# Rows and a column load in the Q stage, statistics turned by VectorE, V's second half, the roots, the index chain and the jump moved: a two-layer kernel on one core

## What is computed

```python
x = x + attn(layernorm(x), Wq, bq, Wk, bk, Wv, bv)
x = x + (einsum('bsi,oi->bso', layernorm(x), weight * scale[:, None]) + bias)
```

```python
q, k, v = heads(h @ Wq + bq), heads(h @ Wk + bk), heads(h @ Wv + bv)
# local: query block i (128 tokens) sees keys i*128-64 .. (i+1)*128+64
ctx = softmax(mask(q_block @ k_window.T / 8)) @ v_window
# global: token 0, the 62 tokens of largest |q| of this head, token 1023
idx = [0, top_k(norm(q), 62), 1023]
ctx[idx] = softmax(q[idx] @ k.T / 8) @ v          # all keys
```

## Time and profile before

| | us |
|---|---|
| median of 3 runs | 2128.19 (2123.09 to 2137.35) |
| profiled execution | 2130.37 |
| its span | 2128.8 |
| TensorE matmuls busy | 2018.6 (95%) |
| VectorE busy | 1521.7 (71%) |
| ScalarE busy | 1002.0 (47%) |
| GpSimd busy | 602.6 (28%) |
| mean granted TensorE clock | 0.970 |

### The profile page before, as it was taken

One profiled execution on the slowest core, in us unless ns is written; L12 is line 12 of the kernel. 1 busy time (PEld: TensorE's weight loads), 2 busy tenths in 40 slices (PEclk: granted clock), 3 DMA queues, 4 the chain that ended last, 5 costly groups with the idle time before them and its releaser, 6 DMA issues.

```text
span 2128.8 us, 36751 instructions
## 1 busy us (share of the span) xinstructions
PE 2018.6 (95%) x11264; PEld 1680.7 (79%) x11264; DVE 1521.7 (71%) x2907; ACT 1002.0 (47%) x1435; POOL 602.6 (28%) x478
## 2 busy tenths in 40 slices
PE   6997999989989999889899998999999989999999
PEld 6875878877868788778687887887888878888887
DVE  5596778763888778637887686578777877666664
ACT  4224756673246666733365666534676672000000
POOL 2332214123342232133422321344223203212121
PEclk9998999989989999899899999999999999999999
DMA  3427787653367767443578775425767656333331
GB/s 139 125 76 147 155 132 164 124 116 114 109 145 166 130 148 155 100 121 114 132 149 131 155 137 125 114 87 117 162 140 181 139 105 190 130 138 128 138 128 69
DMA packets 539685, 280.78 MB, mean 132 GB/s; under 512 B 439120, under 2 KB 504726, under 8 KB 539536
## 3 DMA queue, kind: packets, MB, share of 16 engines
q1 hardware_dynamic: 511440, 186.76, 41.8%
q0 software_dynamic: 23776, 76.63, 12.0%
q10 hardware_dynamic: 4320, 15.73, 1.8%
HBM read 122.73 MB, written 51.44 MB: 82 GB/s over the span
## 4 chain that ended last, share of the span: by engine, by line
PE 77%; DVE 11%; issue 5%; DMA 4%; ACT 2%; SPq 1%; DVEq 0%; POOL 0%; ACTq 0%; POOLq 0%
PE proj L647 39%; PE proj L807 15%; PE pv L765 10%; PE pv L787 3%; PE turn L753 2%; PE score L753 2%; DMA p_turned<-p_parts 2%; DVE top_val L1456 2%; DVE top_idx L1458 2%; DVE x_norm L1460 2%; PE score L779 1%; PE turn L796 1%; DMA v_turned<-q_sq 1%; DVE q_sq L1422 1%; PE proj L925 1%
## 5 line engine op out<-in xcount | busy, mean ns | idle before, releaser
L647 PE MATMUL proj<-xT_hi,w_hi 128*128 128x512 f32 x1536 | 422.3, 419 | 8.9 <-DVE kT_lo L1441 8.8
L647 PE MATMUL proj<-xT_hi,w_lo 128*128 128x512 f32 x1536 | 419.2, 402 | 0.0
L647 PE MATMUL proj<-xT_lo,w_hi 128*128 128x512 f32 x1536 | 383.2, 392 | 0.0
L454 POOL CAST w_hi<-w_raw 128x1024 fp32r<-128x1024 f32 x96 | 108.2, 1127 | 956.6 <-PE proj L647 748.9
L1136 ACT COPY pT<-p_turned 128x1024 uint16<-128x1024 uint16 x256 | 332.0, 1365 | 47.6 <-DMA p_turned<-p_parts 46.6
L647 PEld LDWEIGHTS proj<-xT_hi,w_hi 128*128 128x128 f32 x1536 | 287.7, 197 | 70.5 <-DVE kT_lo L1441 8.1
L647 PEld LDWEIGHTS proj<-xT_lo,w_hi 128*128 128x128 f32 x1536 | 289.4, 188 | 64.2
L647 PEld LDWEIGHTS proj<-xT_hi,w_lo 128*128 128x128 f32 x1536 | 284.8, 192 | 60.6
L765 PEld LDWEIGHTS pv<-v_nat,pT 128*128 128x128 f32 x2048 | 263.1, 203 | 83.5 <-issue 66.5
L765 PE MATMUL pv<-v_nat,pT 128*128 128x65 f32 x2048 | 262.8, 285 | 63.3 <-ACT v_nat L1100 49.0
L1502 DVE COPY p_parts<-probs 128x1024 uint16<-128x1024 uint16 x320 | 246.4, 790 | 99.9 <-DMA p_turned<-p_parts 35.9
(11 more groups left out here) (175 smaller groups left out, 3053.6 us busy)
## 6 DMA issues: line engine op xcount, KB each, us to landing
w_raw<-in_wstream POOLq DMA_DIRECT2D x94, 512.0 KB
x_buf<-in_rows SPq DMA_DIRECT2D x41, 512.0 KB, 4.1
q_rows<-pT SPq DMA_DIRECT2D x64, 256.0 KB
ctx_rows<-ctx_out SPq DMA_DIRECT2D x128, 128.0 KB, 2.4
out<-q_store ACTq DMA_DIRECT2D x30, 512.0 KB, 2.6
q_store<-in_cols POOLq DMA_DIRECT2D x28, 512.0 KB, 5.5
q_store<-ctx_rows SPq DMA_DIRECT2D x28, 512.0 KB
x_buf<-in_rows POOLq DMA_DIRECT2D x14, 512.0 KB, 5.7
```

Source lines behind the costliest of these rows:

```text
L454: pool.tensor_copy(w_hi[b][:, :], w_raw[b][:, :]).then_inc(w_hi_set, 1)
L647: mm = pe.matmul(proj[:, bank, :], w[b][:, k * P:k * P + P], x[:, k, half * HALF:half * HALF + HALF], start=(m == 0), stop=(m == 23), skip ...
```

## The change

- `load_rows(n, 2)` goes out on GpSimd before the index list is stored, that is at the end of the Q stage, and `load_column(n, 0)` before the index columns are loaded; SP's `load_rows(n, 0)` goes behind the first stores of Q.
- The statistics go to memory by another way: VectorE copies means and deviations side by side into 32 columns of `bias_b` (`stat_cols`), turns them in blocks of 32 x 32, and SP writes them with four DMAs of whole rows.
- `row_roots` stage 0 goes from behind `pv_out(u, 1)` to behind step 2's `pv_out(u, 0)`, stage 1 from behind `pv_out(u, 2)` to where stage 0 was; `turn_stats` takes stage 1's place.
- In pair 6 ScalarE takes V's second half out after `join_p(n, hp, 2)` instead of before `join_p(n, hp, 1)`.
- On VectorE `k_lo_out(n, 0, 0)` goes ahead of `top_rows`; `part_v(n, 0, 1)` and `k_lo_out(n, 0, 1)` go behind pair 0's first `maxima`, and two of three top steps from in front of pair 0 into the pairs.
- TensorE's `turn_early_q` of pair 1 and `project_query(n, 2, 1)` go from behind the jump to in front of it (`neck`), with a copy ahead of the loop. Their order among the other instructions stays.

```diff
         bq_c, bk_c, bv_c = sb("bq_c", [P, PAIRS]), sb("bk_c", [P, PAIRS]), sb("bv_c", [P, PAIRS])
         bias_b = sb("bias_b", [P, HID])
+        BLOCK = 32
+        stat_cols, stat_turned = bias_b[:, 0:BLOCK], bias_b[:, BLOCK:2 * BLOCK]
         ln_stats, ln_mv = sb("ln_stats", [P, TILES, 2, 6]), sb("ln_mv", [P, TILES, 2])
         ln_var, ln_bits = sb("ln_var", [P, TILES]), sb("ln_bits", [P, TILES], U32)
...
         rows_loaded = [sem(f"rows_loaded{b}") for b in range(2)]
         last_rows_loaded = [sem(f"last_rows_loaded{b}") for b in range(2)]
-        rows_seen = sem("rows_seen"); sums_set = sem("sums_set"); neg_set = sem("neg_set"); squares_set = sem("squares_set"); stat_set = sem("stat_set"); stat_out = sem("stat_out"); stat_in = sem("stat_in")
+        rows_seen = sem("rows_seen"); sums_set = sem("sums_set"); neg_set = sem("neg_set"); squares_set = sem("squares_set"); stat_copied = sem("stat_copied"); stat_set = sem("stat_set"); stat_out = sem("stat_out"); stat_in = sem("stat_in")
         col_in = sem("col_in"); last_col_in = sem("last_col_in"); col_centred = sem("col_centred"); col_scaled = sem("col_scaled")
         ln_step = sem("ln_step"); xn_set = sem("xn_set")
...
                 sp.wait_ge(stat_set, n + 1)
                 apart(sp)
-                for i, src in enumerate((ln_mv[:, :, 0], ln_rstd[:, :])):
-                    sp.dma_start(stat_rows[n, i].rearrange("(t p) -> p t", p=P), src,
-                                 allow_slow_non_contiguous=True).then_inc(stat_out, 16)
+                rows = stat_rows[n].rearrange("i (t b p) -> b (i t) p", b=4, p=BLOCK)
+                for b in range(4):
+                    sp.dma_start(rows[b], stat_turned[b * BLOCK:b * BLOCK + 2 * TILES, :]).then_inc(stat_out, 16)
             def spread_stats(n):
-                sp.wait_ge(stat_out, n * 32 + 32)
+                sp.wait_ge(stat_out, n * 64 + 64)
                 apart(sp)
                 sp.wait_ge(top_step, (n + 1) * (2 * TOP_LINKS))
...
                 sp.wait_ge(xT_set, n * X_COUNT + X_COUNT)
                 apart(sp)
-                if following:
-                    load_rows(n, 0)
                 for i in range(PAIRS):
                     for h in range(2):
...
                         sp.dma_start(q_tiles[:, 4 * h:4 * h + 4, i * P:i * P + P],
                                      q_nat[:, 4 * h:4 * h + 4, :]).then_inc(q_stored[h], 16)
+                    if following and i == 0:
+                        load_rows(n, 0)
                     if following and i == PAIRS // 2:
                         load_rows(n, 1)
...
                 for what in "vk":
                     split_pair(n, what, 0)
+                if following:
+                    load_rows(n, 2)
                 store_rows(n, 0)
                 split_pair(n, "v", 1)
+                load_column(n, 0)
                 load_columns(n, 0)
                 split_pair(n, "k", 1)
                 gather(n, 0)
-                load_column(n, 0)
-                if following:
-                    load_rows(n, 2)
                 for hp in range(PAIRS - 2):
                     j = hp + 2
...
             def project_q(n, j, norms_too=False):
-                project_query(n, 2 * j, 1)
+                if j > 1:
+                    project_query(n, 2 * j, 1)
                 turn_q(n, 2 * j, 0)
                 if norms_too:
...
                 project_query(n, 2, 0)
-            def rest(n, following):
+            def neck(n):
                 turn_early_q(n, 1, 0)
                 turn_early_q(n, 1, 1)
+                project_query(n, 2, 1)
+
+            def rest(n, following):
                 project_q(n, 1)
                 project_q(n, 2, norms_too=True)
...
                         opening_q(b, quarter, part)
             head(0)
+            neck(0)
             with pe.Fori(0, BATCH - 1) as n:
                 rest(n, True)
                 head(n + 1)
                 global_weigh(n * PAIRS + PAIRS - 1)
+                neck(n + 1)
             rest(BATCH - 1, False)
...
                 for h in range(2):
                     exps(u, 2, h)
-                if not last:
+                if not (early or last):
                     out("v", 1, 2)
                 join_p(n, hp, 1)
...
                 exps(u, 3, 1)
                 join_p(n, hp, 2)
+                if early:
+                    out("v", 1, 2)
                 columns(3)
                 if not last:
...
             dve.memset(batch_base[:, :], 0.0)
             dve.memset(zero_c[:, :], 0.0)
+            dve.memset(stat_cols, 0.0)
             dve.sem_inc(v_parted, V_PIECES)
             dve.sem_inc(p_parted, 2)
...
                     dve.sem_inc(ln_step, 1)
                 roots(FIRST_STEPS + n * LN_LINKS, TILES, stages=(stage,))
-                if stage == 1:
-                    dve.sem_inc(stat_set, 1)
+
+            def turn_stats(n):
+
+                dve.wait_ge(ln_step, FIRST_STEPS + (n + 1) * LN_LINKS)
+                apart(dve)
+                dve.tensor_copy(stat_cols[:, 0:TILES], ln_mv[:, :, 0])
+                dve.tensor_copy(stat_cols[:, TILES:2 * TILES], ln_rstd[:, :]).then_inc(stat_copied, 1)
+                dve.wait_ge(stat_copied, n + 1)
+                apart(dve)
+                dve.transpose(stat_turned, stat_cols).then_inc(stat_set, 1)
             def column_scale(n, i, following):
...
                 maxima(u, 0)
+                if hp == 0:
+                    k_lo_out(n, 0, 1)
+                    part_v(n, 0, 1)
                 top_norms(0)
                 if last:
...
                 if following and hp < HALF_PAIRS - 2:
                     row_moments(n, hp + 2)
+                if following and hp == HALF_PAIRS - 2:
+                    row_roots(n, 0)
                 columns(2)
                 maxima(u, 3)
...
                 pv_out(u, 1)
                 if following and hp == HALF_PAIRS - 2:
-                    row_roots(n, 0)
+                    row_roots(n, 1)
                 columns(3)
                 if ahead:
...
                 pv_out(u, 2)
                 if following and hp == HALF_PAIRS - 2:
-                    row_roots(n, 1)
+                    turn_stats(n)
                 columns(4)
                 if hp == PAIRS - 2 and not following:
...
                         if following and r == 5:
                             row_moments(n, 1)
+                k_lo_out(n, 0, 0)
                 top_rows(n, 0)
-
                 part_v(n, 0, 0)
-                k_lo_out(n, 0, 0)
                 split_q(n * PAIRS, 0)
                 top_find(n, 1, 0)
-                top_find(n, 1, 1)
-                top_find(n, 1, 2)
-                part_v(n, 0, 1)
-                k_lo_out(n, 0, 1)
-                attend(n, 0, 0, range(3, 9), following)
-                attend(n, 1, 0, range(9, 15), following)
-                attend(n, 2, 0, range(15, 21), following)
-                attend(n, 3, 0, range(21, TOP_STEPS), following)
+                attend(n, 0, 0, range(1, 7), following)
+                attend(n, 1, 0, range(7, 13), following)
+                attend(n, 2, 0, range(13, 19), following)
+                attend(n, 3, 0, range(19, TOP_STEPS), following)
                 for hp in range(HALF_PAIRS, PAIRS):
                     attend(n, hp, 1, (), following)
```

## The result

The changed kernel takes 2061.13 us (median of four runs, 2057.03 to 2064.44), the kernel before, timed beside it, 2125.79 us (four runs, 2123.09 to 2137.35). The ratio is 0.9685, with a 95% interval of 0.9642 to 0.9728: 3.1% faster. The forecast was 2027 us, with a range from 2010 to 2062. The sign is right and the size is not: by the medians 65 us are saved, in the profiled executions 2130.4 us became 2058.4, 72 us where 103 were forecast.

What follows compares the result with a forecast made beforehand. TensorE was taken to bound the kernel, at 95% of the span. Savings of 60.6 us of idle and 42.4 us of clock, 103 us together, took 2130.4 us to 2027 us, range 2010 to 2062 us.

Steps and rivals of the forecast that it cites:

- The prediction's own sign of being wrong: A new wait of over 3 us in every batch, most likely in pair 0 or before weigh(6, 2).
- V's half, pair 6: ScalarE's later v_out in pair 6 ends the waits before weigh(6, 1); 22.7 us less 5 left saves 17.7 us.
- statistics and roots: Waits before weigh(3, 0), 11.0 us, and global_weigh, 5.7 us, go; 1 us left, 15.7 us saved.
- pair 0: Moved loads and earlier maxima cut waits of 26.5 us to 3 us in each of four batches, saving 14.5 us.
- end of Q: k_lo_out first frees bank 1 for Q's last part; three waits of 6.4 us go, 1 us left, 5.4 saved.
- jump: Queued weight loads cover TensorE's outer-loop jump; 9.3 us of idle falls to 2, saving 7.3 us.
- work at 0.50, half of it: TensorE's loss at the lower clock falls from 50.9 to 8.5 us, five stretches with 17 us of work; 42.4 saved.
- `part_v(7, 1)` and `pv_out(u, 1)` take VectorE some 1.2 us more: Pair 6, after v_out(7, 1): TensorE then waits about 1.3 us before weigh(u, 2), 3.9 us in three batches.
- Rival (b): Pair 6's wait moves to weigh(u, 2) as part_v(7, 1) blocks VectorE: 3 us more in four batches, 2053 us; chance 0.11.
- Index chain: Two top steps move into pair 3, then five and top_rows (2.2 us) where three were; no wait was priced.
- (d): Pair 0's gather lands late behind loads in GpSimd's queue; slower, 2155 us if 40 us late; chance 0.02.
- (e): The change does nothing: waits from ScalarE's and VectorE's total work come back elsewhere, within 1%, 2120 us; chance 0.03.

Runs made afterwards that it cites:

- stand-in: Either kernel with SP's 416 DMA transposes replaced by plain DMAs of the same tiles: changed kernel 2068.3 and 2061.3 us, kernel before 2118.1 us.
- run 4: Changed kernel's stand-in with GpSimd's split of the next batch's first query slice held until pv_out(6, 1) is done: 2051.9 us, ratio 0.9639.
- run 9: Changed kernel's stand-in with the index chain undone (top_rows and part_v ahead of k_lo_out, top steps back before pair 0): 2051.0 us, ratio 0.9604.
- run 10: Changed kernel's stand-in with part_v(n, 0, 2) moved behind maxima(u, 1) on VectorE in pair 0: 2062.1 us, ratio 0.9696.
- run 8: Changed kernel's stand-in with the loads undone (SP's row tiles ahead of q stores, GpSimd's rows and column back in pair 0): 2080.3 us, ratio 0.9735.
- r_jump_back: Changed kernel's stand-in with turn_early_q and project_query(n, 2, 1) back at the start of the loop's body, behind TensorE's jump: 2070.7 us, ratio 0.9736.
- run 11: Changed kernel's stand-in with four edits: split held, part_v(n, 0, 2) later, V's split before store_rows, top_rows later in pair 3: 2050.0 us, ratio 0.9639.

## Why the prediction was right, and where it was not

Most of the places were right: each wait that the change was said to remove is gone or shorter. Undone one at a time in the stand-in, V's half costs 11 to 18 us, the statistics 23, the loads 19 and the jump 2 to 10; the index chain undone gains 10. The time lies inside the range by 0.9 us, and two of the four runs lie above it. No rival named it either: 2061 us is a sum of several smaller misses, and that they stayed inside was in part luck. The prediction's own sign of being wrong, a new wait of over 3 us in every batch, before `weigh(6, 2)` or in pair 0, is met in three batches of four. The sizes, by the prediction's own terms (us of idle in the profiled executions):

| term | forecast left | measured left | forecast saved | saved |
|---|---|---|---|---|
| V's half, pair 6 | 5 | 10.2 | 17.7 | 12.5 |
| statistics and roots | 1 | 3.4 | 15.7 | 13.3 |
| `weigh(3, 2)`, not in the sum | - | 4.1 | - | -4.1 |
| pair 0 | 12 | 13.1 | 14.5 | 13.4 |
| end of Q | 1 | 3.2 | 5.4 | 3.2 |
| jump | 2 | 0.3 | 7.3 | 9.0 |
| sum | | | 60.6 | 47.3 |
| work at 0.50, half of it | 8.5 | 28.9 | 42.4 | 22.0 |

(The idle time fell by 49.1; the rest are waits under 0.6 us and the start.)

- **Pair 6.** The step that failed is "`part_v(7, 1)` and `pv_out(u, 1)` take VectorE some 1.2 us more". I counted what stands behind `v_out` and not `part_p(6, 3)` ahead of it, at the 0.69 us a copy that the trace of before gives where VectorE had sat idle beside GpSimd's split. Brought forward, its two copies met that split and took 4.31 us, and `weigh(6, 2)` waited 3.2 us in three batches where 1.3 were counted. The prediction priced just this effect for the roots (2.25 us instead of 0.17) and did not ask which other moved piece would meet GpSimd. Rival (b) named the place and nearly the size (3 us more in four batches) with a wrong reason: `v_out` was early, and run 4 removed the wait without touching V's chain.
- **Clock.** "I take five such stretches, 17 us of work" was an analogy to waits of 2 us, and it was read too kindly: "the 2.07 and 1.90 us ones by none" is true of batch 0, but in batches 1 and 2 of the kernel before the same wait for bank 1 (2.18 and 2.20 us) was followed by 3.4 us of work at 0.50 each, at 590.3 and 1023.8 us. Measured are 11 stretches. Of the 20.4 us that were missed, 11.9 stand behind the waits of 2.7 to 3.4 us in pairs 6 and 0, each followed by 3.4 to 6.8 us of work at 0.50 (40.8 us of it, half is 20.4, less the 8.5 granted). The 3 us that the sum itself left in pair 0 were counted as 2 us waits, and the 3 us of pair 6 were not in it. But 1.03 us at 707.6 and 1120.7 us were followed by 3.4 us at 0.50 as well, and 1.03 us at 295.8 us by none. The 2.38 us wait near 1650 us and the 0.87 and 0.73 us near 1691 us were there before and were followed by no stretch then; now they are, with 10.2 us of work. Why the same wait is answered once and not another time stays open; 5 us of the miss hang on it.
- **Statistics and roots.** Right in mechanism. The block transpose takes 0.21 us (0.3 taken). The copy beside it took 1.72 us next to GpSimd's subtraction, `part_p(2, 4)` 2.27 us instead of 1.3; so 1.1 to 1.3 us of the wait before `global_weigh` stay in each batch.
- **Index chain.** "two are added to pair 3, which now has five and `top_rows`" was said, and priced at nothing, because other pairs carry six and a moment pair. `top_rows` stands in one piece right ahead of `part_v` and `pv_out`, though. By run 9 this part as a whole costs the stand-in 10.3 us. The credit of 5.4 us for `k_lo_out` first was hardly a saving there: what TensorE gains there it waits for in `weigh(0, 0)`, 13.5 us against 14.9 in both together.
- **End of Q.** The 2.07 us are gone, as worked out. Next late was not `split_q` but w_lo: GpSimd's split of V's second slice stands behind `store_rows`, which waits for `top_rows`, now later by `k_lo_out`. The list of what is queued behind a delayed piece stopped at VectorE.
- **Pair 0.** 13.1 us against 12. `maxima(0, 1)` was late by the turn of V (4.21 us in front of `part_v(0, 2)`), as in the sum; run 10 shows this chain by removing it. By run 8 the loads act elsewhere than I put them, on the chain to `weigh(0, 2)`; in batch 0 of the kernel before both places waited (9.79 and 4.13 us).
- **Jump.** "no idle if it takes up to 3.3 us" was right in kind. The branch takes 4.07 and 4.13 us, and the 16 weight loads that start while it runs cover all but 0.2 us. The Trainium skill ("Runtime: NRT & Kernel Launch", Instruction fetch mechanics) says that a taken branch out of the pages held forces a fetch before execution goes on; the 3.4 to 7.0 us in every kernel here agree. What it costs is what the work queued on TensorE leaves uncovered. Part of the gain does not come from the move: compared stand-in with stand-in, 7.2 us of idle (3.35 and 3.85) became 4.4 in r_jump_back, where the move is undone; that the row loads no longer lengthen the branch is likely and not shown.
- **Rivals (d) and (e).** The gather was no bottleneck in the changed kernel, but its slack is small: as soon as VectorE came 3.5 us sooner, in run 10, `pad_q` waited 2.48 us for it. The waits did not all come back elsewhere, but of the four mends of run 11 three did.

## What to carry to other kernels

When a wait is removed, price every instruction that is brought forward at its duration beside whatever runs on the other engines at its new time, not at the one it had in a quiet place; here 0.7 us copies became 2.2 us ones next to GpSimd and took up to half of the 31 us that the forecast had too much (9 to 16 us by run 4, clock included). A wait on an engine that is busy for three quarters of the time is often only moved, so follow the chain to the next consumer, over the other engines' queues too, and test the parts one by one: in the stand-in one part of this change cost 10 us where the whole gained 50 to 57. And a stall's length in the trace of before is not its price, since other stalls ahead of it can hide a part (11.0 us of waits seen, 24.5 when it was put back alone). Last, read what followed a wait in every batch before a price is taken from one: the 2 us wait that looked free in batch 0 was not free in the next two.

## What the runs showed of the hardware

- Some of VectorE's instructions get longer beside GpSimd's cast and subtraction of 128x1024, small ones too: a cast of 8x62 elements 2.29 us instead of 0.18, a copy of 128x8 elements 1.72 us (0.16 for its neighbour), two copies of 128x1024 halfwords 4.31 instead of 1.29 us. Others don't: in the changed kernel's trace the 54 maxima of 128x192 beside the subtraction took 0.35 to 0.36 us, as the ten elsewhere did, and 29 FIND_INDEX8 over 8x1024 took 1.21 us, as the others did. So the price depends on the instruction.
- TensorE's backward branch in the outer loop took 3.4 to 7.0 us. It went with the time at which SP had issued two tiles of 512 KB: 5.0 to 7.0 us where the first was issued 1.8 to 2.0 us before it, 3.4 to 4.5 us where it was issued about 5 us or more before it, 3.9 us where it was issued 0.6 to 0.8 us before it. No run varies this time alone.
- A turn by DMA and a plain DMA of the same tile in 254-byte pieces took about the same time on the chain of pair 0: 6.79 and 6.17 us for V, 2.79 and 2.87 us for a P tile.
- A block transpose of 128x32 32-bit elements on VectorE took 0.21 us.
